# Softmax denominators in a decoder layer on one core: reciprocals of one row per head, laid out over all partitions and brought back by DMA

## What is computed

```python
q = (x1 @ wq.T).reshape(b, n, HEADS, HEAD_DIM).transpose(0, 2, 1, 3)   # 16 heads of 32
...
dots = jnp.einsum('bhnd,bhmd->bhnm', q, k) * SCALE
attn = jax.nn.softmax(dots, axis=-1)
out = jnp.einsum('bhnm,bhmd->bhnd', attn, v)
```

## Time and profile before

| | us |
|---|---|
| median of 3 runs (lowest, highest) | 1906.7 (1905.62, 1906.82) |
| the profiled execution, its own time | 1908.03 |
| its span in the trace | 1905.1 |

### The profile page before, as it was taken

How to read it: one execution, slowest core, us unless ns; L and a number is a source line. 1 busy time by engine, 2 the same in 40 slices (tenths; PEclk the granted TensorE clock), 3 DMA queues, 4 the chain that set the end, 5 groups by cost and what they waited for, 6 DMA issues and landing times.

```text
span 1905.1 us, 26591 instructions
## 1 busy us (share of the span) xinstructions
PE 1864.2 (98%) x9972; PEld 1274.0 (67%) x9972; DVE 1252.7 (66%) x2361; ACT 893.1 (47%) x1600; POOL 822.0 (43%) x745
## 2 busy tenths in 40 slices
PE   7999999999999999999999999999969999999998
PEld 6887787788555555555445545544439998899986
DVE  5676564267777788888778778778654444444447
ACT  4312332321666666666456456546724433344333
POOL 4002201100588888888667657666011223212232
PEclk9999999999999999999999999999979999999999
DMA  7003425584757486757644525442234444444544
GB/s 283 23 1 116 166 95 175 205 249 146 157 131 175 106 189 132 163 120 155 138 115 110 134 51 144 112 99 74 84 113 142 138 119 130 108 114 127 149 98 162
DMA packets 124496, 250.10 MB, mean 131 GB/s; under 512 B 11312, under 2 KB 29504, under 8 KB 119680
## 3 DMA queue, kind: packets, MB, share of 16 engines
q1 hardware_dynamic: 109696, 187.56, 33.1%
q0 software_dynamic: 14672, 60.85, 15.6%
HBM read 148.46 MB, written 62.42 MB: 111 GB/s over the span
## 4 chain that ended last, share of the span: by engine, by line
PE 85%; DVE 12%; DMA 1%; issue 1%; ACT 1%; POOL 0%; SPq 0%; DVEq 0%; POOLq 0%; ACTq 0%
PE banks L1192 37%; PE banks L1483 12%; PE banks L1382 11%; PE banks L1352 10%; DVE max L1696 9%; PE banks L1371 9%; PE banks L1403 4%; PE banks L1198 2%; DMA raw<-in_x_t 1%; PE banks L1283 1%; DVE den_c L1715 0%; DMA raw<-in_wk_t 0%; PE banks L1360 0%; DVE src_lo L1547 0%; DMA xg<-x_rows,tok 0%
## 5 line engine op out<-in xcount | busy, mean ns | idle before, releaser
L1696 DVE TENSOR_REDUCE max<-banks 128x1 f32<-128x512 f32 x1024 | 627.9, 682 | 129.3 <-PE banks L1352 128.3
L2200 POOL TENSOR_TENSOR probs<-probs,probs 128x512 f32<-128x512 f32 x464 | 583.4, 1294 | 232.8 <-PE banks L1382 232.8
L2082 ACT ACTIVATE probs<-banks 128x512 f32<-128x512 f32 x1024 | 521.1, 607 | 258.6 <-PE banks L1371 257.9
L1352 PE MATMUL banks<-k_stack,q_stack 98*128 98x512 f32 x1024 | 428.3, 426 | 0.1
L1371 PE MATMUL banks<-q_stack,k_stack 98*128 98x512 f32 x1024 | 376.5, 398 | 2.6 <-ACT probs L2082 2.6
L1352 PEld LDWEIGHTS banks<-k_stack,q_stack 98*128 98x128 f32 x1024 | 191.5, 187 | 192.3 <-DVE max L1696 108.6
L1382 PE MATMUL banks<-probs,v_grp 128*32 128x512 f32 x2048 | 250.6, 602 | 0.0
L1371 PEld LDWEIGHTS banks<-q_stack,k_stack 98*128 98x128 f32 x1024 | 191.7, 188 | 60.1 <-ACT probs L2082 16.8
L2247 POOL DMA_INDIRECT y_rows<-eo,tok x35 | 66.8, 1909 | 172.9 <-DVE eo L1909 100.2
L1896 DVE TENSOR_TENSOR hid_lo<-hid,hid_hi 128x640 fp32r<-128x640 f32 x64 | 52.8, 825 | 127.1 <-ACT hid_hi L2148 127.1
L1382 PEld LDWEIGHTS banks<-probs,v_grp 128*32 128x32 f32 x2048 | 60.0, 109 | 108.6 <-issue 102.5
(11 more groups left out here) (263 smaller groups left out, 2796.6 us busy)
## 6 DMA issues: line engine op xcount, KB each, us to landing
k_stack<-k_parts SPq DMA_DIRECT2D x144, 256.0 KB, 5.1
probs<-probs POOLq DMA_DIRECT2D x36, 1024.0 KB, 9.9
w_raw<-in_L_ffn_w SPq DMA_DIRECT2D x16, 2048.0 KB, 8.2
q_stack<-q_parts SPq DMA_DIRECT2D x48, 256.0 KB
v_grp<-v_rows SPq DMA_DIRECT2D x48, 256.0 KB, 3.2
raw<-in_ctx_t SPq DMA_DIRECT2D x8, 1024.0 KB, 6.3
k_parts<-out_hi SPq DMA_DIRECT2D x32, 256.0 KB, 2.5
k_parts<-out_lo SPq DMA_DIRECT2D x32, 256.0 KB, 2.9
```

The costliest lines, as they stand in the source:

```text
L1352: nc.tensor.matmul(out, queries_of(t)[:, j, tile_of(k)], keys_of(t)[0:STK + SHIFT, j, mc * HALF:(mc + 1) * HALF], start=True, stop=True) \
L1696: V.reduce_max(max4[:, tiles_of(t), :, :][:, k, j, mc:mc + 1], bank(bank_of["max", t, mc, k, j]), AX.X) \
L2082: S.activation(probs_of(t, s)[:, j, :], bank(bank_of["score", t, s, j]), ACT.Exp, scale=SCALE) \
L2200: G.tensor_tensor(a[:, j, :], a[:, j, :], b[:, j, :], ALU.add).then_inc(pair_added.sem, 1)
```

## The change

For turns 0 to 13 the eight reciprocals of 128x64 are replaced by one of 128x16. SyncE spreads one row of each head (512 sums) over the head's 32 partitions of a new tile `den_s`, 16 sums each (four DMAs, block c+1); VectorE takes the reciprocal (c+2); SyncE stores the tile to a DRAM tensor `den_rows` (one DMA, c+2) and reads each head's row back into its 32 partitions of `den_c` (four DMAs, c+3). The multiplies wait for that instead of for the reciprocals, and move to blocks c+5, c+6, c+6 and c+7 (in turn 6 all four to c+5). Turns 14 and 15 stay as they were.

```diff
+SPREAD_DIVISIONS = (5, 6, 6, 7)
...
+        den_rows = nc.dram_tensor("den_rows", (HG, HALF), F32).ap()
...
+        den_s = put("den_s", [P, HG * HALF // P])
...
+        def spread(t):
+
+            return t < LAST - 1
...
+        den_spread, den_stored, den_back = signal("den_spread", HG * 16), signal("den_stored", 16), signal("den_back", HG * 16)
...
                 if s == MT - 1:
                     do("copy_den", t)
+                    if spread(t):
+                        for wait, stage in ((1, "spread_den"), (2, "invert_spread"), (2, "store_den"), (3, "return_den")):
+                            later.append((clock + wait, do, (stage, t)))
+                        for k in range(HT):
+                            later.append((clock + (5 if t == B * NG - 2 else SPREAD_DIVISIONS[k]), divide, (t, k)))
+                        continue
...
+            def invert_spread(t):
+                dve.wait_ge(*den_spread[t])
+                V.reciprocal(den_s[:, :], den_s[:, :]).then_inc(inverted.sem, 1)
...
-                pool.wait_ge(*inverted[t, (k + 1) * SHARE - 1])
+                pool.wait_ge(*(den_back[t] if spread(t) else inverted[t, (k + 1) * SHARE - 1]))
...
+            def spread_den(t):
+                sp.wait_ge(*den_copied[t])
+                for j in range(HG):
+                    Q.dma_start(den_s[j * DH:(j + 1) * DH, :],
+                                den_c[j * DH:j * DH + 1, :].rearrange("r (p f) -> r p f", p=DH)) \
+                        .then_inc(den_spread.sem, 16)
+
+            def store_den(t):
+                sp.wait_ge(*inverted[t])
+                Q.dma_start(den_rows.rearrange("j (p f) -> (j p) f", p=DH), den_s[:, :]).then_inc(den_stored.sem, 16)
+
+            def return_den(t):
+                sp.wait_ge(*den_stored[t])
+                for j in range(HG):
+                    Q.dma_start(den_c[j * DH:(j + 1) * DH, :], den_rows[j].partition_broadcast(DH)) \
+                        .then_inc(den_back.sem, 16)
```

More of the change, by code:

```diff
@@ L453, in program @@
             "invert": lambda t, q: (inverted,),
+            "spread_den": lambda t: (den_spread,),
+            "invert_spread": lambda t: (inverted,),
+            "store_den": lambda t: (den_stored,),
+            "return_den": lambda t: (den_back,),
             "divide": lambda t, k: (divided,),
@@ L1958, in _ @@
                     "xq": lambda *key: split_part("xq", *key), "ctx_k": lambda *key: split_part("ctx_k", *key),
-                    "add_pair": add_pair, "invert": invert, "zero_counts": zero_counts, "rows": rows,
+                    "add_pair": add_pair, "invert": invert, "invert_spread": invert_spread, "zero_counts": zero_counts, "rows": rows,
                     "parts": parts, "row_root": row_root, "row_shift": row_shift, "fold": fold, "fold_turn": fold_turn, "logits": logits,
@@ L2492, in _ @@
                     "ctx_k": ctx_k, "ctx_v": ctx_v, "load_k": load_k, "load_q": load_q, "load_v": load_v,
-                    "one_rows": one_rows, "load_shift": load_shift, "load_fold": load_fold, "load_xwo": load_xwo, "fetch_rows": fetch_rows,
+                    "one_rows": one_rows, "load_shift": load_shift, "spread_den": spread_den, "store_den": store_den, "return_den": return_den,
+                    "load_fold": load_fold, "load_xwo": load_xwo, "fetch_rows": fetch_rows,
                     "fetch_parts": fetch_parts, "x1_logits": x1_logits,
```

## The result

| | before | after |
|---|---|---|
| median of 16 runs each (lowest, highest), us | 1906.16 (1904.92, 1908.71) | 1911.01 (1908.33, 1915.87) |
| ratio, 95% interval | | 1.0025 [1.0018, 1.0031] |
| the profiled execution, us; its span | 1908.03; 1905.1 | 1908.89; 1906.4 |

The account below looks back on a forecast made before the run. TensorE was taken as the bound (85% of the chain, VectorE 12%). Reciprocals removed -3.1, turn 6's spread +1.5, ScalarE's copy +0.2 sum to -1.4 us, giving 1905.3 us; own range 1903 to 1908, with rivals 1901.5 to 1911.5.

Parts of the forecast that it names:

- 3.3 us from twelve blocks: Blocks of turn 8 on, where VectorE delays TensorE: excess removed with the reciprocals, taken as 3.1 us, bounds 0 to 9.6.
- The first rival: VectorE ahead everywhere: more comes off than counted, half to nearly all of 9.6 us, 1902 to 1898.5 us; chance 20%.
- Cost 1.5 us, once: Turn 6: spread queued behind three k_stack loads, VectorE starts the next maxima at about 896.9 instead of 895.33 us.
- the sum: Whole kernel: -3.1 + 1.5 + 0.2 = -1.4 us, giving 1905.3 us.
- the upper bound I had given: Turn 6's wait of VectorE for the spread: counted at 1.5 us, bounds 0 to 3.4.
- so 0: Turn 2, GpSimd multiplying 2.3 us late for the return: 1.8 us of slack remain before ScalarE's fifth exponential, cost 0.
- The limit that I had worked out: Turn 2: GpSimd's late return costs time only once it is more than 1.8 + 2.3 = 4.1 us late at 705.22.
- the third rival: Turns 0, 2, 4 and 6: return too late for GpSimd, sharing engines with the 1 MB DMA; 1913.5 us, chance 14%.
- the 0.2 us that I had counted there: Turn 6: ScalarE's copy of turn 7's denominators waits for four multiplies that come together, 4 x 0.45 us; counted 0.2 us.
- The rival of four spreads served one after another: Turns 8 to 11 and 13: spreads at 1.8 us each end 2.3 us late; about 1914 to 1917 us, chance 5%.
- The 2.0 us that the prediction takes: Fixed part of one DMA; four spreads paid one after another would take 8 us.

Follow-up runs that it names:

- turns 7 to 13 alone: The change applied in turns 7 to 13 only, turns 0 to 6 keeping their eight reciprocals; timed twice against the kernel before: 0.9992 and 0.9994.
- no reciprocals at all: Kernel before without the reciprocals of turns 0 to 13 and without transfers, multiplying by the denominators themselves (not the layer's result): 1905.27 us, 0.9993 of before.
- turns 0 to 5 alone: The change applied in turns 0 to 5 only, against the kernel before: 1908.2 us, ratio 1.0012.
- turn 6's spread a block earlier: The whole change, with turn 6's spread issued in block c instead of c+1, ahead of three key loads: 1906.51 us, 1.0005 of before.
- turn 6 alone: The change applied in turn 6 only, against the kernel before: 1910.87 us, ratio 1.0023.
- the second profile of the change: Profile from timing the changed kernel again, unchanged, against the kernel before: 1911.32 us, ratio 1.0026.
- without turn 6: The change with turn 6 keeping its eight reciprocals, against the kernel before: 1905.95 us, ratio 0.9998.
- the later multiplies: The change without turn 6, multiplies of turns 0 to 5 in blocks c+6, c+6, c+7, c+7: 1905.03 us, 0.9990 of before.

## Why the prediction was wrong

**The gain: right in the blocks, small in the time.** I summed 3.3 us from twelve blocks and took 3.1; eleven blocks are shorter by 2.9. I had not counted that nine others get 0.07 us longer, which leaves 2.3. VectorE's busy time fell by 44.0 us where I had some 50. The one reciprocal takes 0.244 us, forecast 0.25. Over the timed runs the gain is 1.1 to 1.5 us with turns 7 to 13 alone, and 1.3 with no reciprocals at all. What takes the rest is open; the noise of the timings is as large. One thing can be seen: after the loop there is a stretch at the lower clock in every profile. The window of 50 us around it, in the kernel after and with turns 7 to 13 alone:

```profile
1395.00:1445.00 50.00, 34.89 (x186) 25.64 (x175) 27.35 (x89) 15.51 (x22) 11.57 (x14) 0.76 0.54 185
```

```profile
1395.00:1445.00 50.00, 34.52 (x181) 29.27 (x180) 27.52 (x85) 18.63 (x26) 9.98 (x11) 0.73 0.54 183
```

The granted clock is 0.76 in the one and 0.73 in the other: 1.5 us of TensorE's time at full clock (0.03 of 50). Over all twelve profiles it is 0.76 in four (before, after, turns 0 to 5 alone, turn 6's spread a block earlier) and 0.73 in eight, among them turn 6 alone and the second profile of the change. So it differs between executions of one kernel, and it can't be put down to the gain. The first rival (more comes off, up to 9.6 us) is refuted by the kernel with no reciprocals.

**The step that failed: "Cost 1.5 us, once", for turn 6's spread behind three key loads.** The mechanism was right, the place and the line too: VectorE waits 4.94 us where I had some 4, and nowhere else. It was mis-sized twice. The maxima began at 897.76 instead of 896.9. The third key load ahead of the spreads itself landed at 896.8, where I had 896.3, and the last spread 0.7 us behind it. The 0.86 us later come on top of the 1.5 and give about the gap of 2.37 us in TensorE's timeline; not exactly, since the blocks here start 0.4 us earlier than before. (I took the four issues at about 0.5 us each and they took 5.14 us; but the last issue ended at 891.7, 5.9 us before VectorE went on, and whether quicker issues would have landed sooner no run shows.) And the sum had no term for the clock, which falls to 1.2 GHz behind the gap in two of three profiles of this stall and takes 1.6 us and more. Measured in the runs it is 3.8 to 5.1 us; the upper bound I had given was 3.4. This term alone turns a forecast gain into a loss.

**The second step that failed: "so 0" for GpSimd's late multiply in turn 2.** In turns 0 and 2 I had it 0.8 and 2.3 us late; it waits 4.34 and 4.88. In turn 2 I took the landing of one load, 13.8 us after its issue at 693.72, for the whole return. But the issue of the four returns begins at 693.27 and takes 3.84 us, the last goes out at 696.2 and lands 12.9 us later, at 709.1 instead of 707.5; and GpSimd stood ready at 704.3, 0.9 us before the 705.22 that I had. The limit that I had worked out, 4.1 us late, held well: 4.88 is 0.8 beyond it, ScalarE pauses 0.65 and the block gets 0.70 longer; at 3.96, without turn 6, nothing is longer. In the runs the return of turns 0 to 5 costs 1.1 us (without turn 6 against turns 7 to 13 alone, 0.0006, and the same with the later multiplies) to 2.3 us (turns 0 to 5 alone), the first two within the noise, the last clear of it. So the third rival was right in its mechanism and its threshold, but in one of its four turns: turn 0 waited 4.2 to 4.6 us in four profiles without making a block longer (only at 5.38 us was one, by 0.27), and turn 4 did not wait. That the measured 1911.0 lies near its 1913.5 is luck, since most of the loss is turn 6's spread. In turn 6 GpSimd waited 0.51 us, and ScalarE's copy did not wait for the four multiplies: the 0.2 us that I had counted there do not show.

**What was right.** The spreads of turns 7 to 13 land about 3 to 5.5 us ahead of VectorE, turns 1, 3, 4 and 5 get their return in time, and the extra 3.9 MB cost nothing that shows. The rival of four spreads served one after another is false: they land 0.3 to 0.6 us apart, 1.8 to 2.6 us after their issue in turn 10. By the Trainium skill (DMA: Bandwidth & Descriptors, section Rules for kernel authors) transfers under 64 KB pay mostly overhead; here each of 2 KB takes its 1.8 to 2.6 us, but side by side. The same page of the Trainium skill, section Two DMAs through the same engine are not ordered, says that within one queue of one DMA engine the descriptors start in order; the trace shows landings and not starts, but fits: turn 6's four small ones landed only 7.1 to 9.9 us after their issue behind three loads, and within 2.3 us when issued ahead of them. (The 2.0 us that the prediction takes from the Trainium skill's section on the anatomy of one DMA are given there for transfers issued by GpSimd; SyncE issues these.)

**The sum by the runs**: -1.3 (turns 7 to 13) + 3.8 to 5.1 (turn 6) + 1.1 to 2.3 (turns 0 to 5) = 3.6 to 6.1 us; the change took 4.9.

**Open.** Why nine blocks got 0.07 us longer, and what makes the clock's stretches, after a wait and without one, come out differently from execution to execution. Why the issue of a small DMA slows behind large ones, and whether that cost anything, was not tried apart from its place in the queue.

## What to carry to other kernels

A small transfer with a reader close behind costs what stands ahead of it in its queue: place its issue ahead of the large loads, or its reader a block later; each of the two took its part of this loss away. Reckon with the last of a group of DMAs, and with all that stands ahead of it: its issue too slows behind large loads (5.14 us for four, instead of 2.45). A late engine off the critical path costs nothing up to its slack, here 4.1 us, and then at once. And where TensorE is the bound, a stall can cost more than its length because of the clock behind it: here 2.25 us for 1.86, 4.0 for 2.37, 5.4 for 1.95.

## What was not expected of the hardware

- After TensorE gaps of 2.37 and 1.29 us the granted clock fell to the level of 1.2 GHz for a stretch (0.53 over the next 3.60 us, 0.51 over 3.50), after one of 1.95 us for about twice as long (0.50 over 4.00 us in the middle of it); after one of 1.86 us it did not fall. The two executions of the changed kernel show two of these cases. It also fell with no gap: in the profile of before it is 0.84 from 611 to 632 us, where TensorE waits for nobody and does, among others, small matmuls of 8 columns. So a gap is not the whole of what decides it. A profile is one draw: the two of the changed kernel have spans of 1906.4 and 1911.4 us, and the second, at 0.988, a lower mean clock than the first, at 0.991.
- SyncE's issue of one small DMA takes 0.55 to 0.59 us with no large loads just ahead and up to 1.88 us behind three loads of 256 KB.
- The spread from SBUF to SBUF and the broadcast of one DRAM row to 32 partitions are not dear in themselves: 1.8 to 2.6 us to landing for the one in turn 10, 2.8 to 3.2 us for the other in turn 7. While the 1 MB accumulating DMA of turn 2 runs, the same broadcast takes 10.9 to 12.9 us.
